# Normalisation phases of an eight-sublayer kernel: residual additions on GpSimd in groups of four tiles, the inverse root from ACT's square root and DVE's reciprocal, and one order for all engines

## What is computed

```python
def _layernorm(x, axis=-1, eps=1e-05):
    m = jnp.mean(x, axis=axis, keepdims=True)
    v = jnp.var(x, axis=axis, keepdims=True)
    return (x - m) / jnp.sqrt(v + eps)
...
    x = x + _layernorm(_L0_attn_ref(_layernorm(x, axis=-1), ...), axis=-1)
    x = x + _layernorm(_L0_ffn_ref(_layernorm(x, axis=-1), ...), axis=-1)
    ...                                   # six more of the same form
```

## Time and profile before

| | us |
|---|---|
| median of 3 runs | 3142.86 (3142.31 to 3143.49) |
| the profiled execution, its own time | 3144.63 |
| its span, first to last instruction | 3142.3 |
| an addition phase, first statistic to last copy (7 of them) | 18.45 to 18.58 |
| PE, DVE, ACT, POOL busy | 2681.1, 2032.0, 1560.0, 1080.2 |

### The profile page before, as it was taken

One profiled execution on the slowest core, in us unless ns is written; L12 is line 12 of the kernel. 1 busy time (PEld: TensorE's weight loads), 2 busy tenths in 40 slices (PEclk: granted clock), 3 DMA queues, 4 the chain that ended last, 5 costly groups with the idle time before them and its releaser, 6 DMA issues. The chain is left out here.

```text
span 3142.3 us, 54866 instructions
## 1 busy us (share of the span) xinstructions
PE 2681.1 (85%) x21129; PEld 1670.4 (53%) x21149; DVE 2032.0 (65%) x4268; ACT 1560.0 (50%) x3045; POOL 1080.2 (34%) x791
## 2 busy tenths in 40 slices
PE   8985899998839799999999799798877899777798
PEld 4552555566726566666666466465643334335464
DVE  5568899935514555655654666466548999996545
ACT  4334788852413344444444556365457676643122
POOL 3211000001143244443444445055226777773000
PEclk9995899989869899999999799999999999998899
DMA  1000000001120200000000000000013344340000
GB/s 55 1 3 1 2 3 3 3 2 81 35 91 22 92 1 1 1 1 1 1 1 2 28 1 1 1 1 1 1 46 138 136 142 146 136 145 17 1 1 14
DMA packets 35505, 106.72 MB, mean 34 GB/s; under 512 B 3584, under 2 KB 15744, under 8 KB 34480
## 3 DMA queue, kind: packets, MB, share of 16 engines
q1 hardware_dynamic: 32976, 98.49, 9.0%
q0 software_dynamic: 2272, 4.72, 0.4%
HBM read 94.54 MB, written 8.67 MB: 33 GB/s over the span
## 5 line engine op out<-in xcount | busy, mean ns | idle before, releaser
L1926 POOL TENSOR_TENSOR many_probs<-many_probs,many_rinv 128x2048 f32<-128x2048 f32 (+7 forms) x128 | 269.6, 2106 | 361.8 <-DVE many_rinv L1962 361.8
L1005 DVE TENSOR_REDUCE heads_halfmax<-heads_qmajor 128x1 f32<-128x512 f32 x512 | 316.4, 681 | 33.4 <-PE heads_qmajor L866 30.1
L3308 DVE TENSOR_TENSOR_SCAN stream_state<-stream_decay,stream_state 128x512 f32<-128x512 f32 x256 | 306.3, 1233 | 0.5
L970 ACT ACTIVATE weights<-heads_kmajor 128x1024 f32<-128x1024 f32 x256 | 259.2, 1026 | 71.7 <-PE heads_kmajor L878 65.8
L1899 ACT ACTIVATE many_probs<-many_score,many_negmax 128x1024 f32<-128x1024 f32 (+7 forms) x256 | 187.4, 737 | 173.4 <-DVE many_negmax L1946 173.4
L1946 DVE TENSOR_REDUCE many_negmax<-many_score 128x1 f32<-128x1024 f32 (+7 forms) x256 | 184.4, 752 | 111.7 <-PE many_score L1828 110.0
L2978 PE MATMUL stream_yacc<-stream_state,ident 128*128 128x512 f32 x512 | 249.1, 614 | 0.4 <-POOL stream_state L3270 0.4
L3140 ACT ACTIVATE stream_decay<-weights,mamba_negA 128x512 f32<-128x512 f32 x256 | 173.0, 689 | 112.1 <-DVE stream_state L3308 110.8
L3270 POOL TENSOR_TENSOR stream_state<-XN,stream_state 128x1024 f32<-128x1024 f32 x85 | 200.3, 2360 | 80.3 <-DVE stream_state L3308 79.9
L1836 PE MATMUL many_ring<-ident,many_probs 128*128 128x128 f32 x1152 | 174.3, 279 | 23.3 <-POOL many_probs L1926 6.5
L3299 DVE TENSOR_TENSOR stream_state<-stream_bspread,stream_du 128x1024 f32<-128x1024 f32 x128 | 153.2, 1197 | 45.4 <-POOL stream_du L3246 38.8
(11 more groups left out here) (535 smaller groups left out, 5924.8 us busy)
## 6 DMA issues: line engine op xcount, KB each, us to landing
XN<-mamba_crows SPq DMA_DIRECT2D x85, 512.0 KB, 3.6
stream_crow<-mamba_crows SPq DMA_DIRECT2D x43, 512.0 KB, 3.6
weights<-in_w_dram SPq DMA_DIRECT2D x1, 6148.0 KB, 17.3
weights<-in_w_dram SPq DMA_DIRECT2D x1, 4274.0 KB, 13.5
weights<-in_w_dram SPq DMA_DIRECT2D x1, 3296.0 KB, 11.2
swiglu_pairs<-swiglu_fetched SPq DMA_DIRECT2D x1, 2574.0 KB, 11.3
swiglu_fetched<-swiglu_pairs SPq DMA_DIRECT2D x4, 594.0 KB, 6.5
weights<-in_w_dram SPq DMA_DIRECT2D x1, 2112.0 KB, 7.9
```

The source lines that it names most:

```text
L970: nc.scalar.activation(probs_of(k).rearrange("p (a n) -> p a n", a=2), kmajor[:, at:at + 2, :], ACT.Exp, scale=SC).then_inc(exp_done, 1)
L1005: nc.vector.tensor_reduce(halfmax[:, g % 2, at, h % 2:h % 2 + 1], qmajor[:, (2 * n + j) % 3, :], AX, ALU.max).then_inc(max_done, 1)
L1926: nc.gpsimd.tensor_tensor(pair, pair, rinv[:, n % 4, :].unsqueeze(2).broadcast_to([P, 2, wide]), ALU.mult).then_inc(norm_done, 1)
L3308: nc.vector.tensor_tensor_scan(h[:, part(half)], decay[:, (2 * g + half) % DECAYS, :], h[:, part(half)], 0.0 if half == 0 else h[:, BANK - ...
```

## The change

In the norm phases alone: the additions go from DVE (16 of 128x128) to POOL (4 of 128x512), and `x_added` counts groups; the power on POOL is replaced by a `Sqrt` on ACT and a `reciprocal` on DVE; and DVE and ACT both follow one written list `ORDER` of statistics and apply steps. The SP's store waits for groups instead of tiles.

```diff
-        ORDER = sorted(((k, q) for k in range(2) if (add, norm)[k] for q in range(G)),
-                       key=lambda kq: (kq[1] + 2 * kq[0] * add, kq[0]))
+        ORDER = [(k, q, what) for k, q, what in (
+            (0, 0, "statistics"), (0, 1, "statistics"), (0, 0, "apply"), (0, 2, "statistics"), (0, 1, "apply"),
+            (0, 3, "statistics"), (0, 2, "apply"), (1, 0, "statistics"), (0, 3, "apply"), (1, 1, "statistics"),
+            (1, 0, "apply"), (1, 2, "statistics"), (1, 1, "apply"), (1, 3, "statistics"), (1, 2, "apply"),
+            (1, 3, "apply")) if (add, norm)[k]]
...
             def apply(k, q):
+                dve.wait_ge(root_done[k], q + 1)
+                four = slice(4 * q, 4 * q + 4)
+                nc.vector.reciprocal(rstd[:, k, four], rstd[:, k, four]).then_inc(rstd_done[k], 1)
                 dve.wait_ge(rstd_done[k], q + 1)
...
-            def add_group(q):
-                for t in range(4 * q, 4 * q + 4):
-                    wait_normalised(dve, 0, t)
-                    nc.vector.tensor_tensor(m.X[:, t, :], m.X[:, t, :], m.XN[:, t, :], ALU.add).then_inc(x_added, 1)
...
+            for k, q, what in ORDER:
+                if what == "statistics":
+                    statistics(k, q)
+                else:
+                    apply(k, q)
+                    if k == 1 and q >= 2 and q - 2 not in HT_ACT:
+                        copy_out(q - 2)
+            for c in range(2, 4):
+                if norm and c not in HT_ACT:
+                    copy_out(c)
 
         @block.gpsimd
         def _(pool):
-            for k, q in ORDER:
-                pool.wait_ge(var_done[k], q + 1)
-                nc.gpsimd.tensor_tensor(rstd[:, k, 4 * q:4 * q + 4], rstd[:, k, 4 * q:4 * q + 4], m.neghalf[:, 0:4],
-                                        ALU.pow).then_inc(rstd_done[k], 1)
+            for q in range(G if add else 0):
+                for t in range(4 * q, 4 * q + 4):
+                    wait_normalised(pool, 0, t)
+                four = slice(4 * q, 4 * q + 4)
+                nc.gpsimd.tensor_tensor(m.X[:, four, :], m.X[:, four, :], m.XN[:, four, :], ALU.add).then_inc(x_added, 1)
...
+            def root(k, q):
+                act.wait_ge(var_done[k], q + 1)
+                four = slice(4 * q, 4 * q + 4)
+                nc.scalar.activation(rstd[:, k, four], rstd[:, k, four], ACT.Sqrt).then_inc(root_done[k], 1)
...
+            for k, q, what in ORDER:
+                if what == "statistics":
+                    root(k, q)
+                else:
+                    normalise(k, q)
+                    if k == 1 and q - 1 in HT_ACT:
+                        copy_out(q - 1)
...
-                    sp.wait_ge(x_added, (half + 1) * TPB)
+                    sp.wait_ge(x_added, (half + 1) * TPB // 4)
```

More of the change, by code:

```diff
@@ L145, in norm_phase @@
         unread = ph.ps("unread", 1)
-        stat_done, aggr_done, var_done, rstd_done, shift_done, norm_done, own_done = (
-            [ph.sem(f"{s}{k}") for k in range(2)] for s in ("stat", "aggr", "var", "rstd", "shift", "norm", "own"))
+        stat_done, aggr_done, var_done, root_done, rstd_done, shift_done, norm_done, own_done = (
+            [ph.sem(f"{s}{k}") for k in range(2)] for s in ("stat", "aggr", "var", "root", "rstd", "shift", "norm", "own"))
         x_added = ph.sem("x_added")
@@ L172, in statistics @@
                     if k == 1 and add:
-                        dve.wait_ge(x_added, t + 1)
+                        dve.wait_ge(x_added, t // 4 + 1)
                     nc.vector.bn_stats(stats[:, k, t, :], src[k][:, t, :]).then_inc(stat_done[k], 1)
@@ L182, in apply @@
             def apply(k, q):
+                dve.wait_ge(root_done[k], q + 1)
+                four = slice(4 * q, 4 * q + 4)
+                nc.vector.reciprocal(rstd[:, k, four], rstd[:, k, four]).then_inc(rstd_done[k], 1)
                 dve.wait_ge(rstd_done[k], q + 1)
-                four = slice(4 * q, 4 * q + 4)
                 nc.vector.scalar_tensor_tensor(out=shift[:, k, four], in0=mv[:, k, four, 0], scalar=-1.0,
@@ L201, in _, with copy_out @@
[L201 to L216, removed]
+            def copy_out(c):
+                dve.wait_ge(turn_done, 4 * (c + 1))
+                nc.vector.tensor_copy(m.HT[:, c * BANK:(c + 1) * BANK], turned[:, c, :]).then_inc(turn_kept, 1)
@@ L229, in copy_out, with normalise @@
                 nc.scalar.activation(m.HT[:, c * BANK:(c + 1) * BANK], turned[:, c, :], ACT.Copy).then_inc(turn_kept, 1)
-            for k, q in ORDER:
+            def root(k, q):
+                act.wait_ge(var_done[k], q + 1)
+                four = slice(4 * q, 4 * q + 4)
+                nc.scalar.activation(rstd[:, k, four], rstd[:, k, four], ACT.Sqrt).then_inc(root_done[k], 1)
+            def normalise(k, q):
                 act.wait_ge(shift_done[k], q + 1)
@@ L235, in _ @@
                         if k == 1 and add:
-                            act.wait_ge(x_added, t + 1)
+                            act.wait_ge(x_added, t // 4 + 1)
                         nc.scalar.activation(m.XN[:, t, :], src[k][:, t, :], ACT.Identity, bias=shift[:, k, t:t + 1],
                                              scale=rstd[:, k, t:t + 1]).then_inc(norm_done[k], 1)
-                if k == 1 and q - 1 in HT_ACT:
-                    copy_out(q - 1)
+            for k, q, what in ORDER:
[5 more added lines that the diff above has]
+                        copy_out(q - 1)
         @block.tensor
```

## The result

| | before | changed |
|---|---|---|
| median, us | 3142.85 (3140.87 to 3144.61, 12 runs) | 3151.80 (3148.15 to 3153.76, 12 runs) |
| the profiled execution, own time and span | 3144.63, 3142.3 | 3148.22, 3146.4 |
| the seven addition phases together | 129.4 | 133.9 |
| norm0, first statistic to last copy | 10.6 | 11.9 |
| last phase, first statistic to end | 13.56 | 14.88 |

The ratio is 1.0026 [1.0017, 1.0035]: slower, and above the predicted range of 3136.5 to 3150.5. The four last rows add up to the 4.1 us between the two spans (+4.6, +1.3, +1.3, -3.0; the rest is rounding).

What follows compares the result with a forecast made beforehand. Each addition phase was taken as bound by its own chain, with PE setting the pace at the end. Terms -2.1 + 0 + 1.1 - 0.5 = -1.5 gave a median of 3141.4; eight-in-ten range 3136.5 to 3150.5.

Steps and rivals of the forecast that it cites:

- The schedule of norm1 after the change: Addition phase norm1: first transpose at 10.05 against 9.97, DVE's and ACT's work ending 1.2 us sooner; -0.3 in each of seven.
- the fourth addition overtakes tile 0: Rival, addition phases: POOL's addition starts first and holds DVE's tile; +0.85 a phase, total 3149.5; chance 17%.
- over 0.05 longer: Addition phases: the overtaking rival decides when POOL's addition is over 0.05 longer or the reciprocal is.
- Additions of 1.25: Norm phases: each of POOL's 128x512 additions was to take 1.25 us a group.
- some 1.2: Norm phases: DVE's additions were put at 1.2 us a group, so DVE gets rid of 4.8 us.
- Variance steps held at 0.3 to 0.45: Addition phases: DVE's variance steps wait for POOL's addition, taking 0.3 to 0.45 instead of 0.17, three in a phase.
- Both end just behind POOL's: Rows of L2148 (0.81 for 0.17) and L3323 (1.83 for 0.68): both DVE operations end just behind POOL's.
- norm0 at 0: norm0: PE is the pace from 13.12 on, no later tile comes too late; change 0.
- Clock up 3.8 to 5.3 behind the first transpose: Addition phases: PE's clock rise at 3.8 ends the phase at 17.95, at 5.3 at 18.55; 18.2 taken.
- PE cannot use it: Addition phases: DVE and ACT end 1.2 us sooner, but PE starts at the same moment, its stream unchanged.
- The last phase: Last phase: POOL's last addition of 1.25 and ACT's later last tile cost +1.1, bounds 0.8 and 1.5.
- The local transformer: Local transformer: the table load at 1759.06 goes, so the pipeline behind it starts sooner; -0.5, bounds 0 and -1.3.

Runs made afterwards that it cites:

- The wait: Changed kernel, with POOL's fourth addition of an addition phase waiting until DVE has written its own first tile: 3142.05, ratio 1.0003.
- the tile on ACT: Changed kernel, with ACT instead of DVE normalising tile 0 of the second normalisation, no wait added: 3142.57, ratio 1.0004.
- the split: Changed kernel, with POOL's fourth addition of a phase cut into four pieces of 128x128: 3145.52, ratio 1.0013.
- the kernel before with the unread Sqrt: Kernel before, with one unread 128x4 Sqrt at the head of ACT's stream in every norm phase: 3138.06, ratio 0.9991.
- the second profile: Profile of the changed kernel run again without any edit: 3149.07, ratio 1.0024.
- the 40 matmuls: 40 unread matmuls instead of 14 starting each addition phase: kernel before 3140.26, ratio 0.9997; changed kernel with the added wait 3137.63, ratio 0.9988.
- the kernel with the additions alone: Changed kernel with the power left on POOL, plus the added wait and 40 unread matmuls: 3149.88, ratio 1.0022.

## Why the prediction was wrong

**The step that failed** is in "The schedule of norm1 after the change": "DVE's own tile 0 at 9.67 to 10.0. PE's first transpose: 10.05". The tile began at 9.76 and POOL's fourth addition at 9.79, so the order that I worked out was right, and the margin was 0.03, at the low end of the 0.03 to 0.08 that I had. What I took for granted was that the one which starts first by its row is safe, so the sum lets variance steps be held and DVE's own tile not. It is not: DVE, 0.03 us ahead, was held for all of POOL's 1.26, in 14 of 14 phases of two profiles. For 0.03 the rival needed no longer addition and no longer reciprocal. The rival "the fourth addition overtakes tile 0" had mechanism, place and price (first transpose 11.2, a phase 19.35 against a measured mean of 19.13 and 19.39 in the two profiles, total 3149.5 against 3151.8 and 3149.07). Its 17% and its point of decision ("over 0.05 longer") rested on that margin. In the sum the seven phases stood at -2.1; they measured +4.6 and +6.4 in the two profiles. The wait and the tile on ACT take the hold away, the split shortens it, and the first transpose comes to 10.2, 10.3 and 10.4.

The traces show the tile held for the whole POOL instruction: the hold ends 0.08 behind POOL's end, for one of 1.26 and for one of 0.45. ACT is free of it: 1.65 for four tiles beside an addition as without one. Being first by the row did not help: there DVE was ahead by 0.03. What makes DVE wait, no trace here tells.

**Point by point.** Additions of 1.25: 1.26. Additions of a group on DVE, "some 1.2": 0.89 in the trace of before, as at 213.21; the row that I had divided was that of the last phase, in which ACT sets the pace of the additions. So DVE gets rid of 3.6 us, not 4.8, and POOL takes 1.4 times as long as DVE (1.26 to 0.89). That is against DVE's four short additions; against one DVE operation of 128x512 with two inputs it is 1.8 times (1.25 in the earlier trace rows and 0.68 in the earlier trace rows). The prediction had them nearly equal (1.25 and 1.2). Root 0.2 and reciprocal 0.17: as measured. Variance steps held at 0.3 to 0.45: 0.25 to 0.52. Statistics not held: right. "Both end just behind POOL's": wrong for L3323, which ends 0.55 behind, and right for L2148 (0.03), on which the reasoning rests. First root at 1.39 behind the first statistic, table load hidden: right, and the kernel before with the unread Sqrt shows it apart. norm0 at 0: right, the second profile has 10.63. Phases of 17.9 to 18.6: three of fourteen. The low and the high level of the forecast are the granted 0.50 and 0.98 of the earlier trace rows, where its rises at 3.8 and 5.3 stand too; a tile was to take 0.64 and 0.34 at them, and in norm1 of the changed kernel took 0.64 at 0.50 and 0.33 at 1.00. Clock up 3.8 to 5.3 behind the first transpose: 2.7 to 6.1. With the hold gone the sum is nearly met: the kernel with the wait had phases of 18.37 in the mean (forecast 18.2), and 1.0003 of the kernel before, where the forecast was 0.9995. That the mean came so near is in part luck: with the first transpose at 10.16 in all seven, the phases took 17.60 to 19.09, by where the clock fell.

**"PE cannot use it"** holds for a low clock only (granted 0.50). At the high one (1.00) PE used all 0.85 that DVE's chain had gained (17.61 for 18.46). The edit that sells the change is the 40 matmuls, which are worth nothing measurable to the kernel before (0.9997).

**The last phase**, +1.1, measured +1.31: ACT's end and POOL's start lie 0.16 apart, not 0.08; ACT's own end comes 0.17 later, not 0.1; the addition and the store behind it add the last 0.05.

**The local transformer**, -0.5: its first root came 8.37 behind the first copy (1763.60 less 1755.23) instead of 9.90, as the rows of ACT show, of the changed kernel

```profile
1755.23 0.59 ACT L2112 ACTIVATE qkv_HS<-qkv_turned 64x512 f32<-64x512 f32 x1 [8.88 <-PE qkv_turned L2067]
...
1763.60 0.21 ACT L2130 ACTIVATE qkv_root<-qkv_sumsq 128x8 f32<-128x8 f32 x1 [0.40 <-DVE qkv_sumsq L2158]
```

and of the kernel before (its root is in the earlier trace rows).

```profile
1750.45 0.59 ACT L2102 ACTIVATE qkv_HS<-qkv_turned 64x512 f32<-64x512 f32 x1 [8.21 <-PE qkv_turned L2057]
```

Without the load the sublayer took 553.4 to 555.9 in eleven profiles; with it 557.1, 557.1 and, in the kernel with the additions alone, 555.8. So the term is near -2 where -0.5 was forecast (bound -1.3): the first root is 1.5 earlier, of which 1.28 is the load's row; ACT also finds its copy of v 0.6 sooner and then waits 0.4 for the sum of squares, which leaves the other 0.25. How much of the spread is the load's stays open.

## What to carry to other kernels

Before work goes to POOL, list the DVE instructions on the path that will run beside it, and ask which are of the kinds that were held here; a margin of some hundredths of a microsecond between the two is no margin (DVE's tile was 0.03 ahead, and took 1.38 for 0.34). Where one is, put POOL's instruction behind it with a wait, or give the tile to ACT. When a chain gets shorter and the time does not, look at the clock in that stretch: PE's pace can hide the gain until PE is kept busy (with the wait 17.60 to 19.09 a phase, with the 40 matmuls too 17.59 to 17.62).

## What the runs showed of the hardware

- DVE's 128x128 tensor_scalar with two pointers (0.34 alone) was held by POOL's addition in 21 of 21 cases (three profiles) in which its row starts 0.02 to 0.04 us ahead of POOL's; it ended 0.08 behind it each time. Held too: tensor_scalar of 128x4 (up to 1.19 for 0.17), tensor_tensor of 128x128 (four in 1.77 for 0.89), scalar_tensor_tensor of 128x4 (1.11 and 1.22 for 0.16). Not held: the statistics (0.86 for four) and ACT's operations on the same tensors (1.65 for four).
- The hold is for one instruction: beside pieces of 0.45 the tile took 0.57 in all, and the four pieces cost POOL 1.70 instead of 1.26.
- A table load at the head of a phase cost nothing in eight phases: the first root began 0.15 behind its end (210.55 + 1.28 and 211.98), and waited for the variance step, not for the load; it began 0.03 behind that step's end in each of the eight.
- The low clock (granted 0.50) lasted 6.8 us round the first transposes in all seven phases of the kernel before, and 6.8 or 10.2 in the changed kernel (10.2 in five of fourteen); between two profiles of one kernel the seven phases differed by 1.8 us, with all DVE and POOL rows alike.
